# Graph attention on one core: table rows of 65 instead of 128 floats, gathered into two buffers instead of one

## The chip, the core and the metric

The kernel runs on one core of a Trainium2 chip. A time is the device time in microseconds of one execution; for the kernel before, the median of three runs is given. The engines named below are TensorE (PE, its weight loads PEld), VectorE (DVE), ScalarE (ACT), GpSimd (POOL) and SyncE (SP). POOL issues the indirect gathers, in which 128 rows of a table in HBM are fetched by an index for each partition.

## What is computed

A graph has 12500 nodes with 64 channels and 200000 edges, sorted by their target `dst`. Two gated convolutions come first, then two attention layers with batch norm, and layer norms around both pairs. The change is in the attention layers, cut to this:

```python
def gat_conv(x, src, dst, edge_attr, W, We, att_s, att_d, att_e, bias):
    xl = x @ W
    a_src = (xl * att_s).sum(-1); a_dst = (xl * att_d).sum(-1)
    a_edge = ((edge_attr @ We) * att_e).sum(-1)
    alpha = leaky_relu(a_src[src] + a_dst[dst] + a_edge, 0.2)
    ex = exp(alpha - segment_max(alpha, dst)[dst])
    p = ex / segment_sum(ex, dst)[dst]
    return segment_sum(xl[src] * p[..., None], dst) + bias     # self loops left out here
```

For each edge the kernel needs row `xl[src]` (64 floats) and the score `a_src[src]` (one float): 65 floats by index. What depends on `dst` alone is near at hand, since the edges are sorted.

## The kernel before

**Tiling.** The edges are laid out in 1664 steps of 128 edges. A *group* is 4 steps, a *batch* 128 steps or 32 groups, and there are 13 batches. Each stage of the program is a block in which every engine has its own instruction list; the engines meet only through semaphores. `cg_edges` runs twice for the convolutions, `gat_edges` twice for the attention layers. At the end of a stage all engines meet.

**Table and buffer.** `gat_tables` multiplies the nodes by the weights and stores for each node 65 floats (the row and the score `a_src`) in `xl_table`, whose rows are `TW` = 128 floats wide. Columns 65 to 127 are filled once with zeros from `blank` (L585, in the first `cg_edges`), so that a gather of whole rows reads defined values. In `gat_edges` the buffer `buf` holds 128 slots of 128 floats, one slot a step: the rows of one batch.

**One batch on VectorE, ScalarE and TensorE** (`batch` in the three lists). First the softmax for 128 x 128 edges: L1028 takes the near scores (`bank_ad`), L1033 adds the gathered scores (column 64 of all slots, so it waits for the whole batch's gathers, L1031 and L1032), and so on to L1073. Then come the *sums*, 8 iterations of 4 groups. For a group ScalarE weighs the four gathered slots into `msg` (L1148, semaphore `e_m`), VectorE builds a one-hot matrix (L525 for L1082), TensorE multiplies both (L1216, semaphore `e_agg`) and VectorE adds the products to the accumulators (L1096). In between, the near scores of the next batch are *spread*: VectorE builds a bf16 one-hot matrix (L525 for L995), TensorE transposes it (L1165, semaphore `turned`), ScalarE copies it out (L1119), and TensorE multiplies it with `spread_bf` (L1173, semaphore `used`). ScalarE's L1119 waits for these two increments of TensorE alone (L1117, L1118). For batch 0 there is no batch before it, so its spreading is a loop of its own at the start of the stage, `spread_first`, in which nothing depends on POOL.

**What sets the order on POOL.** POOL has one instruction a step, the gather of L976. Before each group of four it waits (L961) until the messages that ScalarE made from the same slots are done: group g of batch b waits for `e_m` to reach (b - 1) x 32 + g + 1. The indices are copied in halves of 64 columns to `idx_stage` (L968, L972), each copy after the gathers that used the old half have landed (L966, L970).

## Time and profile before

| | us |
|---|---|
| median of 3 runs | 12443.34 |
| lowest and highest run | 12418.31, 12456.87 |
| the profiled execution | 12385.3 |
| its span | 12383.6 |
| POOL busy | 6568.8 (53%) |
| TensorE busy, matmuls | 6073.3 (49%) |
| VectorE busy | 4537.0 (37%) |
| ScalarE busy | 3853.0 (31%) |

No engine is busy for the greater part of its time, so shares alone don't name a bound. The first half of the span, to about 6100 us, is setup and the convolutions; from 6189.9 us on it is two attention layers of about 3000 us each. The page names, for each group of instructions, how long the engine stood idle in front of them and what ended it; "issue" is time in which it waited for nothing that the profile shows, "remote" an increment whose sender the profile could not name. A gather that POOL issues is counted as busy only while POOL writes it out, not until the data lands.

### The profile page before, as it was taken

The page shows a single profiled execution, that of the slowest core. Times are in us where ns is not written, and L with a number is a line of the kernel's source. Part 1 is how long each engine was busy: PE and PEld are TensorE (multiplying, and loading weights), DVE is VectorE, ACT ScalarE, POOL GpSimd, SP SyncE. Part 2 cuts the span into 40 slices and gives each one's busy share as a digit, 9 for nine tenths or more (in the row PEclk, how much of TensorE's full clock was granted, in tenths as well). Part 3 has the DMA queues.
Part 4 walks back from the last instruction along what each step waited for, and adds up shares of the span by engine and source line. Part 5 has one row for each costly group of instructions (what it writes and reads, how often), then busy time and mean ns, then how long its engine had stood idle before and what let it go on. Part 6 is the DMA issues. An engine that isn't in the chain of part 4 may idle for free. (4 is left out here: it accounts for less than half of the span.)

```text
span 12383.6 us, 150453 instructions
## 1 busy us (share of the span) xinstructions
PE 6073.3 (49%) x33515; PEld 4947.5 (40%) x33516; DVE 4537.0 (37%) x13059; ACT 3853.0 (31%) x9857; POOL 6568.8 (53%) x6800
## 2 busy tenths in 40 slices
PE   2666666666666666666523333333342333343333
PEld 1444444444444555554413333333332333333332
DVE  5333333333333333333423333333352333333336
ACT  1444434444344444444312222222221222222222
POOL 1555555555455555555355555555515555555551
PEclk6888887887788888878655555555555555555555
DMA  4111111111111111111211111111101111111111
GB/s 117 37 37 38 37 37 37 37 37 37 51 39 38 40 40 39 40 40 39 53 39 39 36 40 38 38 39 36 40 22 39 39 37 38 38 39 40 36 39 31
DMA packets 325714, 498.77 MB, mean 40 GB/s; under 512 B 177366, under 2 KB 214986, under 8 KB 323979
## 3 DMA queue, kind: packets, MB, share of 16 engines
q0 software_dynamic: 214032, 440.06, 13.6%
q1 hardware_dynamic: 106316, 43.62, 1.5%
q10 hardware_dynamic: 5193, 13.44, 0.3%
q14 instruction: 144, 1.18, 0.0%
q8 instruction: 29, 0.48, 0.0%
HBM read 464.28 MB, written 32.36 MB: 40 GB/s over the span
## 5 line engine op out<-in xcount | busy, mean ns | idle before, releaser
L976 POOL DMA_INDIRECT big<-xl_table,idx_stage x3328 | 3268.5, 982 | 2395.2 <-ACT msg L1148 1334.4
L606 POOL DMA_INDIRECT big<-q_table,idx_stage x3328 | 3256.1, 978 | 2400.4 <-PE bank L711 1367.7
L1216 PE MATMUL bank<-msg,onehot 128*128 128x66 f32 x6656 | 1623.5, 426 | 1571.3 <-issue 730.2
L525 DVE TENSOR_TENSOR onehot<-iota,dst_rel 128x512 f32<-128x512 f32 x1664 | 1146.6, 689 | 3020.2 <-remote 1504.1
L1216 PEld LDWEIGHTS bank<-msg,onehot 128*128 128x128 f32 x6656 | 1488.8, 329 | 1732.1 <-issue 984.8
L1096 DVE TENSOR_TENSOR wide<-wide,bank 128x66 f32 x3328 | 732.6, 220 | 3412.2 <-remote 2554.7
L1119 ACT ACTIVATE onehot_t<-bank 128x512 bf16<-128x512 bf16 x832 | 493.8, 594 | 3854.7 <-remote 3196.3
L699 PE MATMUL bank<-ident,onehot 128*128 128x128 f32 x3328 | 697.7, 346 | 2023.2 <-DVE onehot L525 1814.8
L711 PEld LDWEIGHTS bank<-big,onehot_t 128*128 128x128 f32 x6656 | 1176.3, 248 | 621.5 <-issue 621.5
L699 PEld LDWEIGHTS bank<-ident,onehot 128*128 128x128 f32 x3328 | 447.2, 171 | 2139.3 <-DVE onehot L525 1212.3
L708 PE MATMUL bank<-big,ident 128*128 128x512 f32 x1664 | 1248.7, 843 | 26.0 <-DMA big<-q_table,idx_stage 12.4
L711 PE MATMUL bank<-big,onehot_t 128*128 x6656 | 1143.4, 329 | 0.0
L665 ACT ACTIVATE onehot_t<-bank 128x512 f32<-128x512 f32 x832 | 495.6, 596 | 2081.2 <-PE bank L699 1210.1
L1165 PE MATMUL bank<-ident_bf,big 128*128 128x128 bf16 x3328 | 497.2, 305 | 1241.3 <-DVE big L525 981.3
L719 PE MATMUL bank<-msg,onehot 128*128 128x67 f32 (+1 forms) x6656 | 955.8, 294 | 21.4 <-issue 15.3
L719 PEld LDWEIGHTS bank<-msg,onehot 128*128 128x128 f32 x6656 | 949.3, 220 | 23.4 <-issue 16.5
L1148 ACT ACTIVATE msg<-big,work 128x64 f32 (+1 forms) x3328 | 878.6, 337 | 0.1
L648 DVE TENSOR_TENSOR wide<-wide,bank 128x67 f32 (+1 forms) x3328 | 734.9, 221 | 357.8 <-PE bank L719 1.9
L671 ACT ACTIVATE work<-bank 128x512 f32<-128x512 f32 x832 | 496.5, 597 | 1168.3 <-PE bank L711 783.2
L1165 PEld LDWEIGHTS bank<-ident_bf,big 128*128 128x128 bf16 x3328 | 291.9, 130 | 1276.4 <-DVE big L525 1007.0
L525 DVE TENSOR_TENSOR big<-iota,dst_rel 128x512 bf16<-128x512 f32 x832 | 576.1, 694 | 352.8 <-remote 246.0
L676 ACT ACTIVATE work<-work 128x512 f32<-128x512 f32 x832 | 523.9, 630 | 103.4
(214 smaller groups left out, 4591.3 us busy)
## 6 DMA issues: line engine op xcount, KB each, us to landing
big<-q_table,idx_stage POOLq DMA_INDIRECT x3328
big<-xl_table,idx_stage POOLq DMA_INDIRECT x3328
big<-in_edge_attr ACTq DMA_DIRECT2D x12, 1024.0 KB, 4.7
q_table<-wide SPq DMA_DIRECT2D x12, 1024.0 KB, 5.1
xl_table<-big SPq DMA_DIRECT2D x12, 520.0 KB, 4.6
edge_rows<-big SPq DMA_DIRECT2D x1, 3341.0 KB, 11.6
x_dram<-big SPq DMA_DIRECT2D x1, 3136.0 KB, 16.1
out<-big SPq DMA_DIRECT2D x1, 3104.0 KB
```

The costliest lines, as they stand in the source:

```text
L525: return nc.vector.tensor_tensor(to, k.iota[:, :].unsqueeze(1).broadcast_to([P, GROUP, P]), k.dst_rel[:, ds(s, GROUP)].unsqueeze(2).broadc ...
L606: pool.indirect_dma_start(out=ring[:, u, s % GROUP, :], out_offset=None, in_=k.q_table, in_offset=bass.IndirectOffsetOnAxis(ap=k.idx_stage ...
L648: nc.vector.tensor_tensor(to, to, k.psum[4 + c % 2][:, i * P:i * P + width], ALU.add).then_inc(s_add if i < GROUP - 1 else s_acc, 1)
L699: last_one = nc.tensor.transpose(k.psum[c % 2][:, i * P:(i + 1) * P], k.onehot[:, c % UNROLL, i, :], k.ident[:, :])
L708: nc.tensor.matmul(k.psum[2 + j][:, :], k.ident[:, :], ring[:, slot].rearrange("p i c -> p (i c)"), start=True, stop=False)
L711: last_one = nc.tensor.matmul(k.psum[2 + j][:, i * P:(i + 1) * P], k.onehot_t[:, j, i, :], p_tab[:, ds(at[i], 2 * C)], start=False, stop=i ...
L719: last_one = nc.tensor.matmul(k.psum[4 + c % 2][:, i * P:i * P + width], k.onehot[:, c % UNROLL, i, :], k.msg[:, c % UNROLL, i, 0:width], ...
L976: pool.indirect_dma_start(out=buf[:, s, :], out_offset=None, in_=k.xl_table, in_offset=bass.IndirectOffsetOnAxis(ap=k.idx_stage[:, s:s + 1 ...
L1096: nc.vector.tensor_tensor(to, to, k.psum[6 + c % 2][:, i * P:i * P + C + 2], ALU.add).then_inc(e_add if i < GROUP - 1 else e_acc, 1)
L1148: last_one = nc.scalar.activation(k.msg[:, c, i, 0:C], flat(gather[:, ds(s + i, 1), 0:C]), ACT.Copy, scale=flat(wsw[:, ds(s + i, 1), 0:1]))
L1165: last_one = nc.tensor.transpose(turned_bank[c % 2][:, i, :], a_onehot[:, c, i, :], k.ident_bf[:, :])
L1216: last_one = nc.tensor.matmul(k.psum[6 + c % 2][:, i * P:i * P + C + 2], k.onehot[:, c % UNROLL, i, :], k.msg[:, c % UNROLL, i, 0:C + 2], ...
```

## The change

Table rows become 65 floats wide (`TW` = C + 1), so `xl_table` has no unused columns; `blank`, its memset and the fill of L585 with its semaphore are gone. The buffer becomes two buffers of 128 slots of 65 floats, and batch b uses buffer b mod 2. A group's gather now waits for the messages of the batch two before, `(b - 2) * BGROUPS`, which come from the same slots. The rows kept behind the buffer in `big` (`t_row`, `u_row`, `crow`, `a_onehot`) move up from 16384 to 16640 floats. Nothing else changes; the gathers are as many and in the same order.

```diff
-TW = 2 * C
+TW = C + 1
@@ Core, setup
-        self.blank = sb("blank", [P, C])
-            nc.gpsimd.memset(k.blank[:, :], 0.0)
@@ cg_edges
-            if layer == 0:
-                sp.dma_start(k.xl_table.rearrange("(b p) c -> p b c", p=P)[:, :, C + 1:TW],
-                             k.blank[:, 0:TW - C - 1].unsqueeze(1).broadcast_to([P, NB, TW - C - 1])).then_inc(s_blank, 16)
-                sp.wait_ge(s_blank, 16)
@@ gat_tables
-                sp.dma_start(rows[:, b0:b1, 0:C + 1], stage[:, b0:b1, 0:C + 1]).then_inc(s_st, 16)
+                sp.dma_start(rows[:, b0:b1, :], stage[:, b0:b1, 0:TW]).then_inc(s_st, 16)
@@ gat_edges
-    buf = k.big[:, 0:P * TW].rearrange("p (s c) -> p s c", c=TW)
+    buf = [k.big[:, i * P * TW:(i + 1) * P * TW].rearrange("p (s c) -> p s c", c=TW) for i in range(2)]
...
-    at = P * TW
+    at = 2 * P * TW
...
-                        wait(pool, e_m, (b - 1) * BGROUPS + (s // GROUP + 1))
+                        wait(pool, e_m, (b - 2) * BGROUPS + (s // GROUP + 1))
...
-                    pool.indirect_dma_start(out=buf[:, s, :], out_offset=None, in_=k.xl_table,
+                    pool.indirect_dma_start(out=buf[p][:, s, :], out_offset=None, in_=k.xl_table,
...
@@ in batch() of VectorE and of ScalarE
-                gather = buf
+                gather = buf[p]
```

The order of instructions stays; what moves is where POOL waits. POOL's list at the start of an attention layer, before: 128 gathers (L976) without a wait for messages, then batch 1 with a wait for `gat0_e_e_msg` (the semaphore `e_m`) in front of each group of four. `rows0` is the landing of gathers, `gat0_e_idx` the staged indices.

```order
L978 COPY idx_stage<-src_idx 128x64
L976 DMA big<-xl_table,idx_stage 128x128 [waits gat0_e_idx]
L976 DMA big<-xl_table,idx_stage 128x128 x31
L968 COPY idx_stage<-src_idx 128x64
L976 DMA big<-xl_table,idx_stage 128x128 x32
L976 DMA big<-xl_table,idx_stage 128x128 [waits gat0_e_idx]
L976 DMA big<-xl_table,idx_stage 128x128 x31
L972 COPY idx_stage<-src_idx 128x64 [waits rows0]
L976 DMA big<-xl_table,idx_stage 128x128 x32
L976 DMA big<-xl_table,idx_stage 128x128 [waits gat0_e_e_msg,gat0_e_idx]
L976 DMA big<-xl_table,idx_stage 128x128 x3
L976 DMA big<-xl_table,idx_stage 128x128 [waits gat0_e_e_msg]
```

The same place of the changed kernel, from the end of batch 0 on (L970 is its gather, `rows1` and `rows2` are landings):

```order
L970 DMA big<-xl_table,idx_stage 128x65 x32
L970 DMA big<-xl_table,idx_stage 128x65 [waits gat0_e_idx]
L970 DMA big<-xl_table,idx_stage 128x65 x31
L962 COPY idx_stage<-src_idx 128x64 [waits rows1]
L970 DMA big<-xl_table,idx_stage 128x65 x32
L970 DMA big<-xl_table,idx_stage 128x65 [waits gat0_e_idx]
L970 DMA big<-xl_table,idx_stage 128x65 x31
L966 COPY idx_stage<-src_idx 128x64 [waits rows2]
L970 DMA big<-xl_table,idx_stage 128x65 x32
L975 UNCONDITIONAL_BRANCH
```

The first wait for a message has moved from the 129th gather to the 257th, behind the branch into the loop over the later batches.

## Rows read from the trace of the kernel before

**Rows 1.** Page, costliest groups: busy, mean ns | idle before, its main releaser
```profile
L976 POOL DMA_INDIRECT big<-xl_table,idx_stage x3328 | 3268.5, 982 | 2395.2 <-ACT msg L1148 1334.4
```

**Rows 2.** Line L1033, all 26: what it was idle for, us, times
```profile
  DVE onehot_t L1030: 6.1, 20
```

**Rows 3.** Lines L1033 and L976 in four stretches: ns, first and last start
```profile
L1033 DVE TENSOR_TENSOR work<-big,onehot_t x13: 370/372/373, 6398.1 to 9061.2; 128x128 f32<-128x128 f32 x13
...
L1033 DVE TENSOR_TENSOR work<-big,onehot_t x2: 371/372/373, 8842.2 to 9061.2; 128x128 f32<-128x128 f32 x2
...
L1033 DVE TENSOR_TENSOR work<-big,onehot_t x2: 370/372/374, 11930.3 to 12154.3; 128x128 f32<-128x128 f32 x2
...
L976 POOL DMA_INDIRECT big<-xl_table,idx_stage x128: 940/944/1246, 6189.9 to 6349.3; - x128
...
  issue: 38.4, 127
```

**Rows 4.** Timeline, first gathers of layer 0: start, us, engine, line [idle before]
```profile
6267.03 0.61 PE L1165 MATMUL bank<-ident_bf,big 128*128 128x128 bf16 x4
...
6288.11 0.60 ACT L1119 ACTIVATE onehot_t<-bank 128x512 bf16<-128x512 bf16 x1 [21.83 <-remote]
```

**Rows 5.** Timeline after the last of them, and line L1028, all 26
```profile
6349.26 0.94 POOL L976 DMA_INDIRECT big<-xl_table,idx_stage  x1 [0.30 <-issue]
...
6369.38 1.08 ACT L1119 ACTIVATE onehot_t<-bank 128x512 bf16<-128x512 bf16 x2 [13.44 <-remote]
...
6372.55 0.60 ACT L1119 ACTIVATE onehot_t<-bank 128x512 bf16<-128x512 bf16 x1 [0.59 <-PE bank L1165]
...
L1028 DVE COPY onehot_t<-bank x26: 423/424/426, 6396.7 to 12152.9; 128x256 f32<-128x256 f32 x26
```

**Rows 6.** Layer 1: its first gathers by line, and TensorE's timeline after them
```profile
L976 POOL DMA_INDIRECT big<-xl_table,idx_stage x128: 940/944/1362, 9279.6 to 9439.4; - x128
...
9458.56 0.61 PE L1173 MATMUL bank<-spread_bf,onehot_t 128*128 x4 [17.06 <-ACT onehot_t L1119]
...
9460.07 0.63 PE L1173 MATMUL bank<-spread_bf,onehot_t 128*128 x4 [0.36 <-ACT onehot_t L1119]
```

**Rows 7.** Timeline within the sums of two batches of layer 0
```profile
6634.85 1.33 POOL L976 DMA_INDIRECT big<-xl_table,idx_stage  x1 [18.99 <-ACT msg L1148]
...
7187.08 0.94 POOL L976 DMA_INDIRECT big<-xl_table,idx_stage  x1 [5.20 <-ACT msg L1148]
...
7212.49 1.95 PE L1216 MATMUL bank<-msg,onehot 128*128 128x66 f32 x8 [0.72 <-DVE wide L1096]
...
7212.77 0.94 POOL L976 DMA_INDIRECT big<-xl_table,idx_stage  x1 [4.80 <-ACT msg L1148]
...
7215.18 1.94 PE L1216 MATMUL bank<-msg,onehot 128*128 128x66 f32 x8 [0.21 <-issue]
```

**Rows 8.** Setup's gathers: line L250, and timeline
```profile
L250 POOL DMA_INDIRECT wide<-edge_rows,work x13: 942/944/1114, 199.7 to 235.7; - x13
...
207.77 1.09 PE L420 MATMUL bank<-ident,wide 128*128 128x128 f32 x4 [2.87 <-DVE wide L381]
...
208.89 0.28 ACT L316 ACTIVATE dst_rel<-bank 128x128 f32<-128x128 f32 x1 [1.99 <-PE bank L420]
```

**Rows 9.** Windows: us, busy (x) of each engine, PEclk, DMA share, GB/s
```profile
20.00:60.00 40.00, 16.44 (x77) 6.97 (x77) 26.31 (x36) 0.00 (x0) 0.00 (x0) 0.91 0.57 140
...
6200.00:6350.00 150.00, 9.37 (x64) 6.09 (x64) 5.56 (x8) 4.78 (x8) 113.79 (x122) 0.50 0.20 53
```

**Rows 10.** Page's DMA issues (x, KB, us to landing), and two rows of the timeline
```profile
q_table<-wide SPq DMA_DIRECT2D x12, 1024.0 KB, 5.1
xl_table<-big SPq DMA_DIRECT2D x12, 520.0 KB, 4.6
...
297.68 2.08 PE L708 MATMUL bank<-big,ident 128*128 128x512 f32 x2 [5.88 <-DMA big<-q_table,idx_stage]
...
9153.74 0.22 DVE L1254 TENSOR_SCALAR small<-loop_sum 128x98 f32<-128x98 f32 x1 [0.33 <-PEq L950]
```

More of the change, by code:

```diff
@@ L568, in cg_edges @@
     k.row_base = [r + GROUPS // UNROLL * GROUP * 16 for r in row_base]
-    s_turn, s_blank = k.sem(n + "turn"), k.sem(n + "blank")
+    s_turn = k.sem(n + "turn")
     p_tab = k.big[:, 0:NB * 2 * C]
@@ L1128, in batch @@
                 first_group = b * BGROUPS
-                gather = buf
+                gather = buf[p]
                 act.wait_ge(s_x3, b + 1)
```

## The prediction, made before the changed kernel ran

> **What bounds the kernel now.** I read the views from the outside in. The page's table of costly groups first [rows 1]: in the attention half the gathers of L976 are 3328 x 982 ns = 3268 us of POOL, followed by 2395 us in which POOL stood idle, 1334 us of them until a message group of ScalarE (L1148) was made. This is the wait that a second buffer seems to remove. Then what the receiving side waits for [rows 2]: the first vector operation on gathered rows (L1033) was idle 6.1 us in all 26 batches (20 times), and in front of it stands L1030, not a gather. So nobody waits for rows to arrive; POOL waits because the consumers are slow. A batch takes 222 us: the 13 L1033 of layer 0 start from 6398.1 to 9061.2, (9061.2 - 6398.1)/12 = 221.9 [rows 3].
>
> Why the consumers are slow shows best where they have nothing to do with POOL at all. At the start of each layer the engines spread the near scores of batch 0 (L525, L1165, L1119, L1173), while POOL issues the first 128 gathers without a break, one every 1.25 us. TensorE's transposes of a group start at 6267.03 and take 0.61 us; ScalarE, which waits for nothing but TensorE's increments, goes on at 6288.11, after 21.8 us idle [rows 4]. One group each 22.4 us; the trace has seven such steps in a row. When POOL has stopped (6349.26) it takes until 6369.38, then a group needs only 1.2 us (0.59 idle and 0.60 busy on ScalarE at 6372.55) [rows 5]. In layer 1 the same release comes at 9458.56 to 9460.07, for gathers from 9279.6 [rows 6]. From the first gather to the release it is 179.5 us in layer 0 (6369.4 - 6189.9) and 179.5 us in layer 1 (9459.1 - 9279.6, the middle of two steps). 179.5/128 = 1.40 us per gather, against the 1.25 us at which they are issued. I read this as a **hidden queue**: each gather costs 1.40 us somewhere behind POOL, and TensorE's semaphore increments crawl while gathers are queued there. The same number fits the sums: a round of 16 gathers and 4 groups is 25.7 us (7187.08 to 7212.77), 16 x 1.40 = 22.4 plus some 3 us in which TensorE's groups run freely, 2.7 us apart (7212.49, 7215.18) [rows 7]. POOL then waits again, the releases come, and so on: POOL is always right behind the last message it may overwrite.
>
> Is the queue one of bytes or of gathers? In setup, gathers of 514 floats a row (four times the bytes) are 3 us apart, and ScalarE follows TensorE's transposes at once: 207.77 + 1.09, then 208.89 [rows 8]. Plain transfers moved 140 GB/s in one stretch in which TensorE's chain ran at its own pace, against 53 GB/s in the stretch of the first gathers [rows 9]. So it is not bytes; it is indirect gathers issued faster than one in 1.40 us.
>
> **The change, part by part.**
> *Rows of 65 floats.* The gather becomes 128 rows of 260 bytes, still 128 rows and one instruction. POOL's instruction does not depend on the row's length here (944 ns median for 512 bytes [rows 3] and 944 ns for 2056 bytes [rows 8]). I take the hidden 1.40 us as unchanged. Bounds: every 0.01 us of it is worth 3328 x 0.01 = 33 us, either way. If all of it were bytes it would fall with the row to 0.7 us, and issue (1.25 us) would be the limit; setup speaks against that, since 2056 bytes would then need 5.6 us and the gathers there come every 3 us. The line through 1.40 us at 512 bytes and that spacing of 3.0 us, (235.7 - 199.7)/12, at 2056 bytes is the steepest that setup allows: it still lets 260 bytes come down to 1.40 - 252 x 1.6/1544 = 1.14 us. The trace of before can't exclude it. Above, a short row could cost more: for that no row gives a bound, and I allow 0.1 us.
> The Trainium skill, "DMA: Bandwidth & Descriptors", section Specifications, says that transfers below 512 B make the DMA engine read, modify and write, so line rate wants 512 B or more; this speaks against the change. The nearest rows here show no such price: stores of 2048 pieces of 260 bytes landed in 4.6 us, of 2048 pieces of 512 bytes in 5.1 us [rows 10]. By the row the sum stays; if the rule doubled the data time of a gather, it would still be hidden, as the queues are busy a fifth of that stretch [rows 9].
> *The blank fill.* The store of L585 and POOL's memset of 0.15 us go. The fill shares the DMA queues with the first gathers of the first edge stage, whose first consumer waited 5.9 us for them [rows 10]. Worth 0 to 6 us; I take 5 us. The table stores of attention keep their number of pieces: nothing.
> *Two buffers, steady part.* POOL may now overwrite a group when the message two batches back is done. In batches 0 to 10 of each layer POOL starts with both buffers full and follows ScalarE's messages exactly as before, only for rows one batch further on. Same gathers between the same messages, so the same 222 us a batch. Between batches POOL issues its last groups and is then idle 19.0 us until the first message of the next batch, at 6634.85 [rows 7]; this stays, because the hand-over there waits for TensorE's increments and not for rows. The wait of 6.1 us is all that two buffers can give directly.
> *Two buffers, start of a layer.* POOL now issues 256 gathers in a row instead of 128, because no message has to be awaited. The release comes after 256 x 1.40 = 359 us instead of 179.5: +179.5 us. In this time the crawl gets 179.5/22.4 = 8 more groups done, which afterwards need not be done at 1.2 us each: -9.7 us. The first sums start 170 us later in each layer: +340 us. Cover that is gone: none, since the spreading of batch 0 has to be complete before its softmax. If the queue did not grow past 128 gathers, only the issue time would be added: 128 x 1.25 - 7 x 1.2 = 151 us, +302 us.
> *Two buffers, end of a layer.* The last gathers are now issued during batch 10, so batch 11 has POOL silent, as only batch 12 has it today. Batch 12 runs from 9061.2 to the end of its adds at 9153.7, 92.5 us [rows 3, 10]. Batch 11 also spreads scores, a group every 2.7 us: 13.7 us of softmax, 31 x 2.67 = 83 us, 13 us to the next L1033: 110 us. Today it takes 219.0 us in layer 0 (8842.2 to 9061.2) and 224.0 us in layer 1 (11930.3 to 12154.3) [rows 3]. Gain 109 + 114 = 223 us.
> *Layout.* ScalarE and VectorE read rows at a distance of 65 floats instead of 128; L1033 takes 372 ns, and 26 of them matter nothing. L1148 has the same 64 floats in a row.
>
> Sum: +340 - 223 - 5 = **+112 us**, about +0.9%. The profiled execution took 12385.3 us (span 12383.6) and becomes 12497; the median of the runs, 12443.3, lies 58 us above it, and I keep that distance: **12555 us**. With the queue that stops growing it is +74 us, 12517.
>
> **The rivals.**
> *The held increments disappear (faster).* If short rows bring the hidden cost of a gather under the issue time of 1.25 us, nothing queues, TensorE's increments arrive at once, and POOL becomes the bound: 1664 x 1.25 = 2080 us to the last gather, then batch 12 in 92.5 us, 2172 us a layer from its first gather. Today that is 9153.7 - 6189.9 = 2964 us. Twice 790 us less: 10,860 us. It decides at 1.25 us, and the wait of 1334 us would be what the second buffer was for. For it: the line of setup above allows it. Against it: setup and the plain transfers. 8%. A cost between 1.25 and 1.38 us gives 33 us per 0.01 us: some 11,900 to 12,450; 9%.
> The Trainium skill, "TensorE: Matmul & The Clock Gate", section "The cost: per-tile semaphore tail", has an increment of TensorE cost some 26 ns. Applied to this stretch it would mean free increments and the time of this rival; the trace disagrees, with 21.8 us for two of them [rows 4].
> *The start costs nothing (faster).* If the second 128 gathers held nothing up, or the spreading got through while they ran, only the 223 us at the end would be left with a small part of the start: about 12,250. Against it: the crawl did not ease in the first 128. 6%.
> *Dearer gathers (slower still).* Rows that start at any multiple of 4 bytes could need more per row: +33 us per 0.01 us, +330 us at 0.1 us, 12,600 to 12,900. 9%.
> *The change does not do what it says*, POOL held by the index staging (L965 to L974) rather than by messages: those waits were over in advance (38.4 us in all 127 gaps of the first 128, 0.30 us each [rows 3]), so this would show as a start of 128 gathers and no difference: 12,440. 3%.
>
> **How the numbers follow.** Forecast 65%, 12,517 to 12,600 on its own. Against no change a measurement tells about 0.3%, 37 us. Faster: 8 + 9 + 6, less the part of these that is within 0.3%, about 20%. Same: 3% plus the edges of the others, 7%. Slower: 73%. The range goes from 12,240, which takes in the cheap start and the near half of the slightly cheaper gather, to 12,800, which takes in most of the dearer one; the regime change stays outside.
>
> **What would show it.** Right: 256 gathers without a message wait at each layer's start; L1028 first at about 6189.9 + 376 = 6566 (today 6396.7 [rows 5]); periods of L1033 near 222 us in batches 0 to 10 and near 110 us in batch 11; the wait of the gathers for L1148 hardly smaller. Wrong: a crawl step other than 22.4 us, or a release that is not at 1.40 us per gather; then the row's length matters, and the periods of all batches move with it.

## The result, and the profile of the changed kernel

The changed kernel took 12583.66 us (median of 5 runs, 12557.40 to 12640.17), the kernel before 12445.24 us in the same comparison (5 runs, 12418.31 to 12504.73). The ratio is 1.0095, with a 95% interval of 1.0065 to 1.0125: about 1% slower, as forecast (12,555 us). But this holds for the chip of that comparison only. In four later comparisons, on four chips of the same kind, the kernel before took 9,930 to 9,947 us; in one of them the changed kernel was timed too, and there the same change made it 4% faster. The prediction's mechanism is what tells the two places apart, and most of what follows is about that. I call a run **held** where the kernel before took 11,979 us or more beside it, and **free** where it took 9,930 to 9,947 us; nothing lay in between. Free comparisons agree within 0.2%, held ones only within 4% (11,979 to 12,445 us), so two held runs are compared by their attention stages or by their ratios, not by their totals.

First the profile of the changed kernel, which is a held run. Its profiled execution took 12640.17 us (span 12638.4), the slowest of its five. Line numbers are 6 lower than before: L970 is the gather (L976 in [rows 1]), L1142 the message (L1148), L1022 the first copy of the spread scores (L1028), L1027 the first operation on gathered rows (L1033), L1113 ScalarE's copy in the spreading (L1119).

From the page, the group of the gathers and their DMA queue (kind: packets, MB, share of 16 engines):

```profile
q0 software_dynamic: 214032, 332.71, 10.7%
...
L970 POOL DMA_INDIRECT big<-xl_table,idx_stage x3328 | 3268.6, 982 | 2312.5 <-issue 1165.5
```

A quarter of the queue's bytes is gone, and a gather takes POOL 982 ns on average as in [rows 1]. What POOL's gathers waited for, and what L1027 waited for in all 26 batches:

```profile
  issue: 1165.5, 3140
  ACT msg L1142: 1146.2, 187
...
L1027 DVE TENSOR_TENSOR work<-big,onehot_t x26: 377/378/381, 6674.8 to 12409.1; 128x128 f32<-128x128 f32 x26
  DVE onehot_t L1024: 5.8, 19
```

The second buffer was to free POOL from waiting for messages. That wait fell from 1334 us [rows 1] to 1146 us only, and 106 us came back as time between gathers ("issue", 1165.5 against 1059.1 us; 83 us less idle in all). L1027 waits no more for rows than it did in [rows 2].

The start of layer 0, on the timeline (start us, us, engine, line [idle before]):

```profile
6296.31 0.97 POOL L970 DMA_INDIRECT big<-xl_table,idx_stage  x1 [0.80 <-POOL idx_stage L972]
...
6456.98 0.95 POOL L970 DMA_INDIRECT big<-xl_table,idx_stage  x1 [0.30 <-issue]
...
6617.74 0.60 ACT L1113 ACTIVATE onehot_t<-bank 128x512 bf16<-128x512 bf16 x1 [21.91 <-remote]
...
6631.05 0.95 POOL L970 DMA_INDIRECT big<-xl_table,idx_stage  x1 [0.30 <-issue]
...
6638.69 0.60 ACT L1113 ACTIVATE onehot_t<-bank 128x512 bf16<-128x512 bf16 x1 [20.35 <-remote]
...
6639.45 0.62 PE L1167 MATMUL bank<-spread_bf,onehot_t 128*128 x4 [19.76 <-ACT onehot_t L1113]
...
6655.60 1.08 ACT L1113 ACTIVATE onehot_t<-bank 128x512 bf16<-128x512 bf16 x2 [16.31 <-remote]
...
6671.85 0.60 ACT L1113 ACTIVATE onehot_t<-bank 128x512 bf16<-128x512 bf16 x1 [0.62 <-PE bank L1159]
...
6673.46 0.42 DVE L1022 COPY onehot_t<-bank 128x256 f32<-128x256 f32 x1 [3.87 <-PE bank L1167]
```

At 6456.98, where the kernel before had to stop, POOL goes on; its 256th gather starts at 6631.05. ScalarE's copies are 22 us apart as in [rows 4] until the release at 6655.60, and 1.2 us apart after it. The release is 359.3 us after the first gather (in [rows 4, 5]: 179.5 us), L1022 377.2 us after it. Layer 1 does the same, from 9473.04 to 9849.76, 376.7 us:

```profile
9473.04 0.97 POOL L970 DMA_INDIRECT big<-xl_table,idx_stage  x1 [1.10 <-issue]
...
9849.76 0.42 DVE L1022 COPY onehot_t<-bank 128x256 f32<-128x256 f32 x1 [3.92 <-PE bank L1167]
```

It is TensorE's increments that come late, and not everybody's: at 6638.69 ScalarE copies for 0.60 us, and TensorE goes on at 6639.45, 0.16 us after the copy. The trace also keeps the times at which semaphore increments were recorded. In the kernel before, TensorE's multiplication that ended at 6267.10 has its increment at 6277.59, 10.5 us later, and the transposes that ended at 6267.64 have theirs at 6288.09, 10.5 us after that one; the increments of ScalarE and VectorE in the same stretch stand 0.01 us behind their instructions. So one step of the crawl, 22.4 us, is two increments of TensorE of 10.5 us each, one behind the other, and some 1.4 us of work.

What they stand in line behind is not data. The kernel before issues its last gather without a wait at 6349.26; this is the busy share of the DMA engines from 6350 to 6370 us, in slices of 0.5 us:

```profile
DMA  0220000000000000000000000000000000000000
```

By 6351.5 the last row has arrived, and TensorE's increments are held until 6369.38 all the same. The packets of each of the first 128 gathers of layer 0 are through about 2.2 us after its issue, in this held run and in a free run of the same kernel alike.

The batches, by L1027 in four stretches (first and last start; x12 are batches 0 to 11, x2 are batches 11 and 12 of layer 0 and then of layer 1), beside [rows 3]:

```profile
L1027 DVE TENSOR_TENSOR work<-big,onehot_t x12: 378/380/381, 6674.8 to 9142.6; 128x128 f32<-128x128 f32 x12
...
L1027 DVE TENSOR_TENSOR work<-big,onehot_t x2: 378/380/381, 9142.6 to 9251.4; 128x128 f32<-128x128 f32 x2
...
L1027 DVE TENSOR_TENSOR work<-big,onehot_t x12: 377/378/381, 9851.1 to 12301.4; 128x128 f32<-128x128 f32 x12
...
L1027 DVE TENSOR_TENSOR work<-big,onehot_t x2: 378/379/380, 12301.4 to 12409.1; 128x128 f32<-128x128 f32 x2
```

Batches 0 to 10 take 2467.8/11 = 224.3 us and 2450.3/11 = 222.8 us, batch 11 takes 108.8 and 107.7 us.

### The profile page after: what moved, and what is told of

The parts are those of the page before. It is cut to its first block and busy times, and to the rows that moved or that the text cites. A ratio compares the mean times of both kernels' runs of the same rounds, so it can differ in the third digit from the quotient of the medians.

```text
span 12638.4 us, 150450 instructions
## 1 busy us (share of the span) xinstructions
PE 6051.6 (48%) x33515; PEld 4933.2 (39%) x33516; DVE 4542.1 (36%) x13059; ACT 3855.9 (31%) x9857; POOL 6573.0 (52%) x6799
## 5 line engine op out<-in xcount | busy, mean ns | idle before, releaser
L970 POOL DMA_INDIRECT big<-xl_table,idx_stage x3328 | 3268.6, 982 | 2312.5 <-issue 1165.5
L1113 ACT ACTIVATE onehot_t<-bank 128x512 bf16<-128x512 bf16 x832 | 494.2, 594 | 4020.9 <-remote 3298.5
L1142 ACT ACTIVATE msg<-big,work 128x64 f32 (+1 forms) x3328 | 879.6, 337 | 0.1
L1167 PEld LDWEIGHTS bank<-spread_bf,onehot_t 128*128 128x128 bf16 x3328 | 345.1, 149 | 808.5 <-issue 800.3
```

What stands on the lines that cost most here:

```text
L970: pool.indirect_dma_start(out=buf[p][:, s, :], out_offset=None, in_=k.xl_table, in_offset=bass.IndirectOffsetOnAxis(ap=k.idx_stage[:, s:s ...
L1142: last_one = nc.scalar.activation(k.msg[:, c, i, 0:C], flat(gather[:, ds(s + i, 1), 0:C]), ACT.Copy, scale=flat(wsw[:, ds(s + i, 1), 0:1]))
```

## The experiments

Each kernel ran beside the kernel before on the same chip, and the first lines of each result say what the kernel before took there. Where one time is given for a kernel, it is a single run. "Layer" below is the stretch from a stage's first gather to its last message.

### Rows of 65 floats alone

```diff
-TW = 2 * C
+TW = C + 1
-                sp.dma_start(k.xl_table...[:, :, C + 1:TW], k.blank...).then_inc(s_blank, 16)
-                sp.wait_ge(s_blank, 16)
-                sp.dma_start(rows[:, b0:b1, 0:C + 1], stage[:, b0:b1, 0:C + 1]).then_inc(s_st, 16)
+                sp.dma_start(rows[:, b0:b1, :], stage[:, b0:b1, 0:TW]).then_inc(s_st, 16)
```

> The kernel before with rows of 65 floats and without the blank fill; one buffer of 128 slots and the wait for the messages of the batch before stay. Theory (the gathers are paid for by number, 1.40 us each behind POOL, whatever their bytes): the fill's 5 us go and nothing else, 12,440 us, L1033's period stays at 222 us. Rival (bytes or row length count, either way): 0.01 to 0.03 us more a gather for rows under 512 bytes gives 12,475 to 12,540; a queue that drains faster with half the bytes gives batches under 215 us, so 12,250 or less. The two together with the doubled buffer would otherwise hide behind each other in the change.

Free: before 9936.33 us (13 runs, 9925.64 to 9951.84), this 9937.98 us, ratio 1.0002, interval 0.9992 to 1.0011. Layer 0's batches take (7122.3 - 4925.7)/12 = 183.1 us, and the kernel before, in its own free run below, has 183.0 us. What L1027 waited for in layer 0:

```profile
L1027 DVE TENSOR_TENSOR work<-big,onehot_t x13: 377/378/380, 4925.7 to 7122.3; 128x128 f32<-128x128 f32 x13
  DMA big<-xl_table,idx_stage: 984.6, 13
```

Half the bytes of the attention gathers change nothing within 0.1% of the kernel's time in a free run. Held, this kernel was not run. The 5 us of the blank fill can't be seen (0.05%). The surprise is the other number: the kernel before is 2,500 us faster here, and L1027 waits 76 us a batch for its rows, for which it waited not at all in [rows 2]. (In the traces of the kernel before, 1,030 us of it lie in the two attention layers and 1,400 us in the two CG stages, the gated convolutions of `cg_edges`, which gather 1664 times each as well.)

### Where TensorE's increments are not held

The changed kernel and the kernel before, unchanged, once more.

> The changed kernel as it is, once more, beside the kernel before. In the first four experiments the kernel before took 9,936 us instead of 12,445 us, and none of TensorE's increments was held: the spreading went at 1.2 us a group under 128 queued gathers, and a batch took 183 us. Theory, mended (the change costs time only where TensorE's increments are held while gathers are queued): where the kernel before takes 9,936 us, nothing is held, the second buffer lets POOL issue without waiting for messages, batches take 128 x 1.26 + 5 = 166 us instead of 183 us, and the layer's start costs nothing: 9,540 us, a ratio of 0.96. Where the kernel before takes 12,445 us the first result returns: 12,584 us, a ratio of 1.01. Rival (the change costs time by itself, by the start of the layer): a ratio of 1.0 to 1.01 in either place.

> The kernel before, for its trace in this place. Mended theory: where it takes 9,936 us, ACT's copies of the spreading in layer 0 follow each other by 1.2 us from the first gathers on, the first L1028 ends some 50 us after the first gather and then waits for the gathers, L1033's period is 183 us. Where it takes 12,445 us, everything is as in the first profile: copies 22 us apart, L1033's period 222 us. No third state between the two is expected.

Free: before 9930.22 us (7 runs, 9924.96 to 9935.94), the changed kernel 9525.29 us (4 runs, 9520.89 to 9531.19), ratio **0.9595**, interval 0.9579 to 0.9611. The kernel before's start of layer 0 there, on the timeline:

```profile
4801.52 0.60 ACT L1119 ACTIVATE onehot_t<-bank 128x512 bf16<-128x512 bf16 x1 [1.16 <-PE bank L1165]
...
4801.89 1.17 POOL L976 DMA_INDIRECT big<-xl_table,idx_stage  x1 [0.30 <-issue]
...
4802.00 0.61 PE L1165 MATMUL bank<-ident_bf,big 128*128 128x128 bf16 x4
...
4802.65 0.60 ACT L1119 ACTIVATE onehot_t<-bank 128x512 bf16<-128x512 bf16 x1 [0.53 <-PE bank L1165]
```

The same instructions as in [rows 4], between the same gathers 1.25 us apart; here ScalarE goes on 0.04 us after TensorE's transposes end, there 20 us after, and TensorE's increments stand 0.01 us behind their instructions. A window of this stretch, to be laid beside the second one of [rows 9] (us, busy (x) of PE, PEld, DVE, ACT, POOL, PEclk, DMA share, GB/s):

```profile
4780.00:4930.00 150.00, 36.80 (x256) 24.16 (x256) 30.03 (x48) 19.10 (x32) 114.01 (x122) 0.50 0.20 52
```

Granted clock 0.50 (1.2 GHz, the lower of TensorE's two levels), DMA share 0.20, 52 against 53 GB/s and 122 gathers in both: only that ScalarE made 32 copies here and 8 there. So the clock isn't what makes the difference in this stretch.

The records of the increments differ too. Each gather adds 16 to its semaphore, once for each of its 16 packets of data, 26,624 times in a layer. For layer 0 the trace has 26,575 records of these increments in the free run of the kernel before and 5,407 in its held run, though it has all 26,624 data packets in both.

In this free run, the waits of layer 0's gathers are, for the kernel before and then for the changed one,

```profile
  issue: 481.5, 1592
  ACT msg L1148: 227.5, 71
```

```profile
L970 POOL DMA_INDIRECT big<-xl_table,idx_stage x1664: 940/945/1470, 4759.0 to 6908.9; - x185
  issue: 491.5, 1622
  ACT msg L1142: 11.5, 41
```

and this is the wait that the second buffer removes: POOL stops after each batch until the first new message,

```profile
4939.64 0.94 POOL L976 DMA_INDIRECT big<-xl_table,idx_stage  x1 [0.31 <-issue]
4957.88 1.18 POOL L976 DMA_INDIRECT big<-xl_table,idx_stage  x1 [17.29 <-ACT msg L1148]
```

and the changed kernel doesn't. Its L1027 start from 4922.2 to 6911.9, 165.8 us a batch instead of 183.0. 24 batches x 17.2 us = 413 us; measured 405 us. The mended theory holds and its rival falls: the change is worth 4% where nothing is held, and it cost 1% in the comparison where TensorE's increments were held.

### A wait before batch 1's gathers

```diff
                         wait(pool, e_m, (b - 2) * BGROUPS + (s // GROUP + 1))
+                        if isinstance(b, int) and b == 1 and s == 0:
+                            pool.wait_ge(spread_sems[0][3], BGROUPS)
```

> The changed kernel, but POOL waits once before its gathers of batch 1 until the spreading for batch 0 is released on TensorE (all 32 groups expanded). Theory (TensorE's increments come free only when the queue of gathers, 1.40 us each, is drained): the spreading is released after 128 x 1.40 = 179 us instead of 359 us, the first L1022 stands 195 to 200 us after the first gather instead of 377 us, and POOL starts batch 1 some 20 us after it would have ended batch 0. The start gives back about 160 us a layer; batch 1's gathers are then under way during batch 0 as in the kernel before, so some of the 110 us that batch 11 saved stays: 12,584 - 2 x 160 = 12,260 us, 12,200 to 12,350. Rival (the start costs because the gathers of batch 1 have to be finished for another reason, or the batch after pays the delay back): 12,500 to 12,600.

> The changed kernel with POOL's one wait before batch 1's gathers, until batch 0's spreading is released (the same kernel as in the first four). Where the kernel before takes 9,930 us: 9,530 us again. Where it takes 12,000 us or more, theory: release after 128 x 1.40 = 179 us instead of 359 us, the first L1024 some 200 us after the first gather, 160 us less a layer, a ratio of 0.985 to the kernel before (0.975 to 0.995) instead of 1.01. Rival (the delay is paid back in the next batches, so that the start isn't what made the change slower): a ratio of 1.00 to 1.015.

Both free: 9537.56 us (ratio 0.9598, interval 0.9582 to 0.9614) and 9531.84 us (before 9936.77). The changed kernel without the wait took 9525.29 us. Nothing is to be gained there, since the spreading is done 49 us after the first gather. Neither run says anything of the held start; the run of both layers below does.

### A short pause after each gather of the attention stages

```diff
                     pool.indirect_dma_start(out=buf[p][:, s, :], ...).then_inc(s_gat[p][half], 16)
+                    for r in range(3):
+                        nc.gpsimd.memset(k.pause[:, r, s, :], 0.0)
```

> The changed kernel with three one-column memsets on POOL after each of the 3328 gathers of the attention stages, so that they are issued some 1.5 us apart instead of 1.25 us; nothing else changes, and the output is the same. Theory (TensorE's increments are held while a queue behind POOL grows, at 1.40 us a gather): above 1.40 us no queue grows, no increment of TensorE is held, the spreading is released in under 60 us, the steps of the batches no longer cost 10.5 us each, and the layers are bound by POOL alone: 13 x 128 x 1.52 us + 110 us = 2640 us a layer instead of 3040 us, so 11,750 to 11,850 us. Slower issue makes the kernel 750 us faster. Rival (increments are held as long as any gather is under way, or by the transfers themselves): batches stay at 222 us or grow with the spacing, 12,550 to 12,900.

> The same with one memset after each gather: issue some 1.34 us apart, still under 1.40 us. Theory (a threshold at 1.40 us): the queue still grows, by 0.06 us a gather, and TensorE's increments are still held most of the time; batches of 205 to 222 us, the start released after some 350 us, 12,300 to 12,600 us. Rival (what matters is any idle time on POOL, in proportion): a third of the gain of the kernel with three memsets.

Both free: 9584.03 and 9535.33 us, where both expectations are for a held chip. The kernels missed their spacing too: one small memset takes 0.12 us here and three take 0.18 us, which slips nearly whole into the 0.3 us that pass between two gathers anyway. One left a batch at 166.0 us (165.8 without), three made it 168.0 us. They show only that POOL is the bound in a free run: 26 x 2.2 us = 57 us, and 59 us were measured against the changed kernel's 9525.29 us.

### The DMA engines kept busy

```diff
             k.clear_old(sp)
+            for i in range(30):
+                sp.dma_start(k.scratch.rearrange("(r f) c -> r (f c)", f=8), k.q_table.rearrange("(r f) c -> r (f c)", f=8)).then_inc(s_load, 16)
+                sp.wait_ge(s_load, 16 * (i + 1))
```

> The changed kernel, and beside it SP copies q_table (6.4 MB, dead by then) 30 times within DRAM in rows of 4 KB during each attention stage, one copy after the other, so that the 16 DMA engines are no longer free for the gathers. It is meant to make each gather cost more than POOL's 1.26 us, where the undisturbed chip has it below. Theory (TensorE's increments are held whenever gathers queue up behind POOL, for whatever reason the queue is slow): while the copies run, ACT's copies of the spreading in layer 0 come 10 to 25 us apart instead of 1.2 us, POOL's spacing grows to 1.3 to 2 us, and the batches under load take over 200 us. Rival A (a slow queue delays only the gathers): POOL's spacing and the batches grow, but the copies of the spreading stay 1.2 us apart. Rival B (queues of this kind do not meet): everything stays at 166 us a batch, 9,525 us. Where the kernel before takes 12,445 us, the copies make the held state worse: over 12,900 us.

Held: before 11979.02 us, this 12083.41 us, a ratio of 1.009, that of the change without any load. Three windows of layer 0 (columns as above), during the start, in batch 0, and in batch 4, when the copies were over; and ScalarE's copies under load:

```profile
5830.00:6150.00 320.00, 18.89 (x131) 12.15 (x129) 11.11 (x16) 9.55 (x16) 233.01 (x247) 0.50 0.97 309
6200.00:6390.00 190.00, 78.49 (x507) 72.31 (x505) 60.52 (x183) 50.56 (x187) 121.61 (x125) 0.50 0.95 306
7100.00:7300.00 200.00, 73.13 (x451) 64.53 (x451) 66.45 (x211) 46.23 (x167) 108.98 (x113) 0.50 0.12 19
```

```profile
5908.22 0.60 ACT L1117 ACTIVATE onehot_t<-bank 128x512 bf16<-128x512 bf16 x1 [21.11 <-remote]
...
L1026 DVE COPY onehot_t<-bank x1: 425/425/425, 6184.1 to 6184.1; 128x256 f32<-128x256 f32 x1
```

309 GB/s at a DMA share of 0.97, against 24 GB/s at 0.13 in the same stretch of the changed kernel; the rows of the first 128 gathers are all there 16 us after the last issue instead of 2 us, and the copies are still 22 us apart; L1026 (L1022 there) comes 370.7 us after the first gather (5813.4), and batches 0 and 1 take 219 and 218 us like the unloaded ones. Half of my expectation was wrong: I thought the hidden queue was one for the DMA engines, which a load would make slower. In a held run it is not: some thirteen times the traffic adds nothing. That agrees with the DMA engines being idle for the last 18 us of the hold in the kernel before, and that gathers, not bytes, are paid for is shown more sharply than by [rows 9]. What is compared here is the attention stage of two held runs on different chips, and batches with and without load in one trace. Whether a load could bring the holding about on a free chip was not tried.

### A pause after all gathers, long enough

```diff
                     pool.indirect_dma_start(...).then_inc(...)
+                    wait(pool, s_pause, b * P + s)
+                    pool.sem_inc(s_turn, 1)
+                    nc.gpsimd.memset(k.pause[:, :], 0.0).then_inc(s_pause, 1)    # 128 x 280, CG and attention stages
```

> The changed kernel with one memset of 128x280 and a wait for the one before it after each of the 6656 gathers (CG and attention stages), so that POOL issues them some 1.47 us apart, 0.21 us slower than by itself and above the 1.40 us that a gather costs behind POOL where TensorE's increments are held. Theory (they are held only while gathers queue up): nothing is held in either place, POOL alone sets the time, 9,525 + 6656 x 0.21 = 10,920 us wherever it runs: 12% faster than the kernel before where that takes 12,000 to 12,450 us, 10% slower where it takes 9,930 us. There the first L1022 comes 50 us after the first gather in both places. Rival (they are held whenever a gather is under way, or by another cause of that chip): where the kernel before takes 12,000 us or more, batches stay at 215 us or more and the CG stages get no shorter, 12,000 to 13,500 us.

Free: before 9936.77 us, this 11232.37 us. The spacing became 1.48 us in the first batch and 1.57 us in the others, more than meant, and POOL's time carries the whole difference to the 9525.29 us of the changed kernel (10,920 us were expected): the CG stages are 404 and 403 us longer than in its free run, the attention layers 441 and 463 us, 1,711 us in all against 1,707 measured. The stretch of the first batch stays free, its L1029 49 us after the first gather. The time where increments are held, for which the kernel was made, this run can't tell.

### Gate in one layer, pause in the other

The wait of the third experiment in attention layer 0 alone, the pause of the last one in the CG and attention stages of layer 1 alone.

> One trace for two questions, since the stages of layer 0 and layer 1 do the same work: the changed kernel with POOL's one wait before batch 1 (until batch 0's spreading is released) in attention layer 0 alone, and with the pause after each gather (some 1.5 us between gathers) in the CG and attention stages of layer 1 alone. Lengths are from a stage's first gather to its last gather (CG) or last message (attention). Where the kernel before takes 12,000 us or more, theory: CG layer 0 takes 2,670 to 2,900 us and CG layer 1, though its gathers are issued more slowly, only 2,540 us; attention layer 0 takes 2,830 to 2,890 us instead of 2,985 to 3,050 us, its first L1024 200 us after the first gather; attention layer 1 takes 2,700 us with its first L1022 50 us after the first gather. Rival (a slower issue can't free TensorE's increments, the start isn't the price): CG layer 1 2,670 us or more, both attention layers 2,985 us or more. Where the kernel before takes 9,930 us nothing is held anyway, and only POOL's issue shows: CG 2,130 and 2,540 us, attention 2,240 and 2,700 us.

> The kernel of the run before once more, for a chip on which TensorE's increments are held. Where the kernel before takes 12,000 us or more, theory: CG layer 0 2,670 to 2,900 us and CG layer 1, paced, 2,540 us; attention layer 0, gated, 2,830 to 2,890 us instead of 2,985 to 3,050 us, its first L1024 some 200 us after the first gather; attention layer 1, paced, 2,700 us with its first L1022 50 us after the first gather. Rival: CG layer 1 2,670 us or more, both attention layers 2,985 us or more. Where the kernel before takes 9,930 us: 10,390 us again.

The first came to a free chip: before 9945.79 us, this 10390.56 us, as expected there. The second was **held** (before 12055.05 us), and took 11743.06 us, a ratio of 0.974. This is the run that settles the mechanism. The CG gathers of layer 0, without pause, and of layer 1, with it (x1664: ns, first to last start):

```profile
L601 POOL DMA_INDIRECT big<-q_table,idx_stage x1664: 938/944/1443, 284.1 to 2997.8; - x185
  PE bank L710: 527.1, 171
...
L601 POOL DMA_INDIRECT big<-q_table,idx_stage x1664: 949/950/7302, 3071.6 to 5604.4; - x185
  PE bank L710: 14.0, 10
```

The attention layers: L1038 (L1027 in the changed kernel) and the messages, of layer 0 and of layer 1:

```profile
L1038 DVE TENSOR_TENSOR work<-big,onehot_t x13: 377/378/380, 5956.9 to 8677.1; 128x128 f32<-128x128 f32 x13
  DVE onehot_t L1035: 2.1, 10
...
L1153 ACT ACTIVATE msg<-big,work x1664: 331/337/352, 5970.6 to 8758.9; 128x64 f32 x162, 128x64 f32<-128x64 f32 x23
  POOL big L977: 637.9, 88
...
L1038 DVE TENSOR_TENSOR work<-big,onehot_t x13: 377/379/381, 9089.2 to 11512.1; 128x128 f32<-128x128 f32 x13
  DMA big<-xl_table,idx_stage: 1163.6, 13
...
L1153 ACT ACTIVATE msg<-big,work x1664: 331/337/349, 9103.5 to 11593.9; 128x64 f32 x162, 128x64 f32<-128x64 f32 x23
```

The pause: POOL issues each gather later, and both stages get shorter, the CG stage 2532.8 us instead of 2713.7 us, the attention layer (from 8899.1) 2694.8 us instead of 3009.1 us (from 5749.8). In layer 1 nobody waits 638 us for messages any more, and L1038 waits for rows as on a free chip: 90 us a batch. The free run with the same pause has 2701.0 us for this layer. Only the first L1033 stayed behind, 76.1 us after the first gather where 50 us were expected. So on a held chip the paced stages run nearly as on a free one, with gathers about 1.5 to 1.6 us apart. A chip that changed its condition midway doesn't explain it, since the four stages ran in the order held, paced, held, paced; nor do the pause instructions as such, since the next run has them, only shorter, and is held. The increments are held by the rate of gathers, and the rival (held whenever a gather is under way) falls.

The records of landings follow: 5,251 of 26,624 in attention layer 0, and 20,640 in the paced layer 1.

The gate: with it, L1033 (L1022 in the changed kernel) starts at 5955.5, 205.7 us after the first gather, as expected. But nothing is won: the layer takes 3009 us, not the 2830 to 2890 us expected; the load run, which has no gate, has 2985 us. After the gate POOL issues batch 1 without a stop and batch 2 with stops of 54 us in all, and TensorE's increments are held then instead:

```profile
L977 POOL DMA_INDIRECT big<-xl_table,idx_stage x128: 940/944/1222, 5956.3 to 6115.9; - x128
  PE bank L1178: 45.5, 1
...
6130.10 0.60 ACT L1124 ACTIVATE onehot_t<-bank 128x512 bf16<-128x512 bf16 x1 [43.94 <-remote]
...
L1153 ACT ACTIVATE msg<-big,work x128: 332/337/343, 5970.6 to 6321.7; 128x64 f32 x112, 128x64 f32<-128x64 f32 x16
```

Batch 0's messages take 351.1 us; in the load run, without gate, 186.3 us (6199.1 to 6385.4). 165 us saved at the start (370.7 - 205.7), 165 us lost in batch 0. Here the rival written down with the first gate was right.

### Pauses on either side of 1.40 us

The edit is shown against the kernel with the pause of 128x280 in all four stages.

```diff
-                    nc.gpsimd.memset(k.pause[:, :], 0.0).then_inc(s_pause, 1)
+                    nc.gpsimd.memset(k.pause[:, 0:60 + 100 * layer], 0.0).then_inc(s_pause, 1)
```

> The changed kernel with a pause after every gather as in the runs with 128x280, but smaller, on either side of 1.40 us: memsets of 128x60 in the stages of layer 0 (gathers some 1.38 us apart on average in the attention stage, 1.33 us in the CG stage) and of 128x160 in those of layer 1 (1.47 and 1.42 us). Where the kernel before takes 12,000 us or more, theory (a threshold at 1.40 us): attention layer 0 stays near 3,000 us (2,850 to 3,050) with batches of 210 us or more, attention layer 1 takes 2,540 us (to 2,620) with batches of 188 to 193 us; CG layer 0 2,600 to 2,900 us, CG layer 1 2,370 to 2,500 us; 11,300 to 11,500 us in all. Rival (each us of pause helps in proportion, no threshold): attention layer 0 already down to 2,750 us or less. Where the kernel before takes 9,930 us, only POOL's issue shows: attention 2,390 and 2,540 us, CG 2,220 and 2,370 us, 10,300 us.

Held: before 11994.62 us, this 12270.03 us, a ratio of 1.023, where 11,300 to 11,500 us were expected. The spacing missed its aim again in layer 1: 1.42 us in the first two batches instead of 1.47 us. The CG stages took 2979.5 and 2626.1 us (2,600 to 2,900 and 2,370 to 2,500 expected); what they take on this chip without a pause isn't known, and elsewhere they took 2673.5 to 2917.9 and 2627.3 to 2887.5 us held.

```profile
L974 POOL DMA_INDIRECT big<-xl_table,idx_stage x129: 949/950/1416, 9410.6 to 9592.2; - x129
...
L1034 DVE TENSOR_TENSOR work<-big,onehot_t x13: 378/380/381, 6377.9 to 9007.6; 128x128 f32<-128x128 f32 x13
...
L1034 DVE TENSOR_TENSOR work<-big,onehot_t x13: 378/378/381, 9413.1 to 12039.1; 128x128 f32<-128x128 f32 x13
```

(129 gathers in 181.6 us.) So both layers are still on the held side, and layer 1 does not tell what 1.47 us would have done. With the other runs it makes a scale for the start of a layer. An early L1022 alone isn't a gain, as the gate showed: what is saved there can be paid back in batch 0. So the table also has the second L1027, which starts batch 1:

| run | spacing of the gathers, first and second 128 | first L1022 after the first gather | second L1027 after it | layer |
|---|---|---|---|---|
| changed kernel, layer 0, held | 1.26 and 1.37 us | 377 us | 601 us | 3037 us |
| gate, layer 0, held | 1.26 and 1.26 us, the second from 206 us on | 206 us | 591 us | 3009 us |
| this, layer 0, held | 1.39 and 1.43 us | 261 us | 564 us | 2974 us |
| this, layer 1, held | 1.42 and 1.42 us | 173 us | 556 us | 2891 us |
| pause 128x280, layer 1, held | 1.48 and 1.57 us | 76 us | 391 us | 2695 us |
| pause 128x280, layer 1, free | 1.48 and 1.57 us | 49 us | 392 us | 2701 us |
| changed kernel, layer 0, free | 1.26 and 1.30 us | 49 us | 329 us | 2235 us |

The rival in its strict form (every us of pause helps in proportion) wanted layer 0 at 2,750 us or less and falls. At 1.42 us the first L1022 comes in half the time, but batch 0 then takes 373.0 us, so that batch 1 starts only 45 us earlier than without a pause, and batches 1 to 10 take 214 us each. At 1.48 and 1.57 us batch 1 starts when it does on a free chip. So the edge lies between 1.42 us and some 1.5 us, and a pause that stays below it gains the attention layers 2 to 4% here against the changed kernel's first comparison (3037 and 3018 us), not the 11% of the longer one.

## Why the prediction came out right, point by point

**What bounds the kernel.** "Each gather costs 1.40 us somewhere behind POOL, and TensorE's semaphore increments crawl while gathers are queued there." The price is confirmed by the release at 359.3 us for 256 gathers (1.40 us each), by the pause, which frees the increments by slower issue, and by the load, which shows that it isn't bytes. "While gathers are queued there" was wrong: the gathers are through 2.2 us after their issue, and the increments stay held for 18 us after the last of them. What is queued is something that the gathers leave behind. (The crawl in [rows 4] was also miscounted: seven of ScalarE's copies make six steps, of which the last five are 22.4 us.) What I had not seen is that this is a condition of the chip at the time and not of the kernel. Nothing in the trace of before could say so, for it held the crawl everywhere that gathers came at full rate.

**Rows of 65 floats: 0.** Right, 1.0002 in a free run; for a held run there is no such pair, but the hidden cost itself stayed, 359.3/256 = 1.40 us with rows of 260 bytes and 179.5/128 = 1.40 us with 512 bytes. The rule of the Trainium skill that I weighed there ("DMA: Bandwidth & Descriptors", Specifications, at least 512 B a transfer for line rate) would have shown in POOL's spacing or in L1027's wait for rows, had it mattered to these gathers, and did in neither: 984.6 us with rows of 260 bytes, 985.9 us with 512 bytes.

**Blank fill: -5 us.** Not measurable (0.05%).

**Steady batches: unchanged.** Nearly. Measured from L1027 of batch 0 to L1027 of batch 11, layer 0 takes 2467.8 us against 2444.1 [rows 3], layer 1 2450.3 us against 2442.3: 32 us more that the sum doesn't have. It need not be the change: under the load, also held, the changed kernel's batches took 220.2 and 220.8 us on average, less than the 222 us of the kernel before.

**Start of a layer: +170 us each.** The size was right to the us: 377.2 - 206.8 [rows 5] = 170.4 us in layer 0, 169.8 us in layer 1. The bound for a queue that doesn't grow past 128 gathers (151 us) was not met. POOL itself took longer for the second 128 gathers, 174.1 us (6457.0 to 6631.0) instead of 159.4 us; in the free run they took 164.7 us. What the reasoning had too narrow is why it is paid at the start. The gate shows that the price hangs on the gathers and not on the place: 128 gathers that wait for no message are 128 x 1.40 us in which TensorE gets nowhere, at the start of a layer or in batch 0 alike.

**End of a layer: -223 us.** 108.8 against 219.0 us and 107.7 against 224.0 us: -226.5 us. The forecast of 110 us for batch 11 was taken from TensorE's free pace, and that holds.

**The sum.** +340 - 226 + 32 = +146 us for the two layers from first gather to last message: 3036.9 + 3018.0 us against 2953.1 + 2956.5 us, +145 us. Forecast +117 us without the fill. The profiled executions differ by 255 us; 106 us of the rest lie ahead of attention, whose first gather starts at 6296.3 instead of 6189.9, after CG stages that the change doesn't touch. The forecast for the profiled execution, 12,497 us, was 143 us low, that for the median, 12,555 us, 29 us low. That the median came so close is partly luck, since stages that the change leaves alone moved by nearly as much as its whole effect; what speaks for the mechanism is that the start and the end of the layers each came within 4 us of their terms.

**The rivals.** The first one described the free chip well and for a wrong reason. I gave it 8%, as a thing that shorter rows might do, with 2172 us a layer; the changed kernel's layers took 2235 us where nothing is held, and there the kernel before, with one buffer, takes the same time with long and short rows. What is wrong in this rival is that it holds the kernel before fixed. Where the increments are free, the kernel before is not at 12,443 but at 9,930 us, and the gain is 4%, not 13%. The other rivals didn't occur.

**What the runs leave open.** What puts a chip into either condition. Of eight comparisons four were free and four held; one and the same chip was free in the run with the pause everywhere and held in the second run of the kernel with gate and pause. All runs of one comparison agreed (9925.64 to 9951.84 us in 13 runs; 12418.31 to 12504.73 in 5). And what the queue is was not seen directly. It isn't ahead of the DMA engines, whose last packet ends 18 us before the release. That leaves what follows a gather, and the trace has a rival there that no run tests: the records of increments. They are nearly complete in a free layer (26,575 of 26,624), thin out where TensorE is held (5,407), and come back with the pause (20,640). It may be the writing of these records that TensorE's increments wait behind, in which case the held condition would be one of the recorded execution. Every execution on record comes with the profiler's span and clock, so none shows what either kernel takes without them.

## What to carry to other kernels

Before you remove a producer's wait, ask what the producer does with its freedom: the buffer that lets gathers run ahead was worth 17 us a batch where TensorE's increments were free, and cost 1.40 us for each gather that ran ahead where they were held. When an engine is late for increments that were made long ago, compare its idle time with the same instructions in a stretch without the suspected traffic, then try a slower issue; if that makes a stage shorter, it is the rate that counts. And have the kernel before timed in more than one place before you trust a difference of 1%: here the sign of the change depends on it, and none of these kernels is best in both (the changed kernel with 9,525 us where it is free; a pause that spaces the gathers 1.5 us or more where it is held: an estimate of some 11,230 us, if all four stages took what the paced ones took in the held run; that wasn't run). And ask of a wait that only some executions show whether it belongs to the program or to its recording, before you build a kernel around it; here that stays open.

## What the runs showed of the hardware that I had not expected

- The same program took 9,930 to 9,947 us in some comparisons and 11,979 to 12,445 us in others, on one core, at the same granted clock of 0.50 in the attention stages. The engine that waits for TensorE's increments went on 0.04 us after the matmuls' end in one (4802.00 + 0.61 to 4802.65) and 20.5 us after it in the other [rows 4], while 128-row gathers were issued 1.25 us apart. Nearly all of the 20.5 us is two increments of TensorE, one behind the other and 10.5 us each; those of ScalarE and VectorE were 0.01 us behind in both.
- Issuing them 1.57 us apart instead of 1.25 us made a held stage 10% shorter (2694.8 against 3009.1 us, the latter with the gate). Spacings of 1.39 to 1.43 us were still held (batch 1 started 556 and 564 us after the first gather, 601 us without a pause), 1.48 to 1.57 us no longer (391 us).
- Some thirteen times the DMA traffic (309 against 24 GB/s) neither slowed POOL's gathers (256 in 333.7 us; 334.7 us without) nor TensorE's increments further.
- In the second 128 of 256 gathers POOL's own spacing rises from 1.26 to 1.37 us on average in a held run, and to 1.30 us in a free one.
- The held increments outlast the gathers: the DMA engines were done by 6351.5, the increments free at 6369.38. The trace has 5,407 of the 26,624 records of landings in that layer, and 26,575 in the same layer of a free run.
- A memset of one column on POOL takes 0.12 us, three take 0.18 us, and they are hidden nearly whole in the 0.3 us between two gathers.
